# A fourth key block of the last batch moved from the projections into attention unit 3

## What is computed

```python
q = _heads(hidden_states @ to_q_w)
h_txt = _sdpa(q, _heads(ehs_txt @ to_k_w), _heads(ehs_txt @ to_v_w))
h_obj = _sdpa(q, _heads(ehs_obj @ to_k_object_w), _heads(ehs_obj @ to_v_object_w))
h_oth = _sdpa(q, _heads(ehs_oth @ to_k_others_w), _heads(ehs_oth @ to_v_others_w))
h_ip = _sdpa(q, _heads(ehs_ip @ to_k_ip_w), _heads(ehs_ip @ to_v_ip_w))
out = _merge(h_txt) + _merge(h_obj) + _merge(h_oth) + _merge(h_ip)
out = out @ to_out_w + to_out_b
out = (out + residual) / RESCALE
```

## Time and profile before

| what | us |
|---|---|
| median of 3 runs | 2387.88 (2387.11 to 2392.84) |
| the profiled execution | 2389.89 |
| its span | 2387.9 |
| PE busy | 2370.0 |
| ACT busy | 1777.2 |
| DVE busy | 1833.7 |
| POOL busy | 412.3 |

### The profile page before, as it was taken

The page is one execution under the profiler, slowest core; times in us unless marked ns, Lnnn a source line. Parts: engine busy times, 40 slices in busy tenths (PEclk is TensorE's granted clock), DMA queues, the critical chain, the costliest instruction groups (busy, mean ns, idle before and its releaser), DMA issues.

```text
span 2387.9 us, 37663 instructions
## 1 busy us (share of the span) xinstructions
PE 2370.0 (99%) x12801; PEld 1804.1 (76%) x12801; DVE 1833.7 (77%) x3291; ACT 1777.2 (74%) x3906; POOL 412.3 (17%) x564
## 2 busy tenths in 40 slices
PE   9999999999999999999999999999999999999999
PEld 8999999998999986566666666666666666666665
DVE  4457777632333479999999999999999999999994
ACT  4333433332222369999999999999999999999995
POOL 0000000000000023313223133133132232231310
PEclk9999999999999999999999999999999999999999
DMA  9545444385654577757777677676676776675762
GB/s 339 164 129 153 150 144 133 108 268 160 222 177 162 185 166 149 150 129 150 150 142 151 130 150 159 131 150 150 130 160 143 138 150 144 147 156 124 146 132 77
DMA packets 371750, 370.12 MB, mean 155 GB/s; under 512 B 110047, under 2 KB 298591, under 8 KB 371559
## 3 DMA queue, kind: packets, MB, share of 16 engines
q1 hardware_dynamic: 334384, 306.14, 56.2%
q10 hardware_dynamic: 37174, 61.59, 7.1%
HBM read 215.57 MB, written 83.89 MB: 125 GB/s over the span
## 4 chain that ended last, share of the span: by engine, by line
PE 96%; ACT 1%; DMA 1%; SPq 1%; issue 0%; DVE 0%; POOL 0%; ACTq 0%; POOLq 0%
PE st_ps L1660 17%; PE s_ps L489 13%; PE st_ps L509 12%; PE om_ps L523 12%; PE om_ps L544 11%; PE om_ps L567 10%; PE s_ps L1712 7%; PE om_ps L1712 4%; PE s_ps L1680 3%; PE st_ps L1712 3%; DMA qpack<-q_out 1%; PE om_ps L1729 1%; ACT s_ps L689 1%; PE om_ps L602 1%; ACT probs L681 1%; DMA xs_raw<-in_xT 0%
## 5 line engine op out<-in xcount | busy, mean ns | idle before, releaser
L689 ACT ACTIVATE s_ps<-s_ps,negmax 128x427 f32<-128x427 f32 x1280 | 768.1, 608 | 21.0 <-DVE small L758 20.9
L749 DVE TENSOR_REDUCE negmax<-s_ps 128x2 f32<-128x854 f32 x640 | 665.3, 1040 | 83.5 <-PE s_ps L489 77.1
L681 ACT ACTIVATE probs<-st_ps 128x1024 f32<-128x1024 f32 x632 | 656.3, 1038 | 21.9 <-PE st_ps L509 9.4
L489 PE MATMUL s_ps<-kpack,qpack 96*128 96x512 f32 x1280 | 422.2, 411 | 5.0 <-DMA qpack<-q_out 3.3
L509 PE MATMUL st_ps<-qpack,kpack 104*128 104x512 f32 x1264 | 404.9, 401 | 3.4 <-ACT probs L681 3.3
L447 POOL TENSOR_TENSOR small<-small,negmax 128x616 f32<-128x616 f32 x160 | 196.4, 1227 | 990.1 <-DVE negmax L766 990.0
L1660 PE MATMUL st_ps<-ctx_split,w_split_ip 128*128 128x428 f32 x1848 | 364.2, 357 | 0.0
L489 PEld LDWEIGHTS s_ps<-kpack,qpack 96*128 96x128 f32 x1280 | 223.6, 189 | 182.1 <-ACT s_ps L689 80.3
L1660 PEld LDWEIGHTS st_ps<-ctx_split,w_split_ip 128*128 128x128 f32 x1848 | 347.0, 188 | 15.6 <-issue 1.0
L544 PE MATMUL om_ps<-xs,wq 128*128 128x512 f32 x1200 | 342.6, 395 | 0.4 <-POOL xs L438 0.3
L567 PE MATMUL om_ps<-heads,wo 128*128 128x512 f32 x1125 | 320.7, 393 | 0.0
(11 more groups left out here) (116 smaller groups left out, 2436.8 us busy)
## 6 DMA issues: line engine op xcount, KB each, us to landing
qpack<-q_out SPq DMA_DIRECT2D x240, 256.0 KB, 6.8
kpack<-kT SPq DMA_DIRECT2D x240, 217.5 KB, 3.4
kT<-k_out ACTq DMA_DIRECT2D x154, 217.5 KB, 3.5
ctx_split_raw<-in_ctxT SPq DMA_DIRECT2D x128, 214.0 KB, 4.6
tok_pair<-in_ctxT SPq DMA_DIRECT2D x48, 512.0 KB, 4.7
xs_raw<-in_xT SPq DMA_DIRECT2D x85, 256.0 KB, 4.2
out<-in_xT SPq DMA_DIRECT2D x75, 256.0 KB, 4.8
out_yT<-out SPq DMA_DIRECT2D x75, 256.0 KB, 2.1
```

The source lines that it names most:

```text
L489: last = nc.tensor.matmul(s_ps[:, n % 2, z, :], qpack[r][0:ROWS_S, j, t * P:(t + 1) * P], kpack[r][0:ROWS_S, j, :], start=True, stop=True)
L681: nc.scalar.activation(probs[:, at:at + 2, :], transposed(u, duo), ACT.Exp).then_inc(p_done, 1)
L689: last = nc.scalar.activation(s_ps[:, n % 2, z, SMALL:TOK], s_ps[:, n % 2, z, SMALL:TOK], ACT.Exp, bias=negmax[:, r, IP, j, t:t + 1], accu ...
L749: nc.vector.tensor_reduce(negmax[:, r, IP, j, t0:t0 + 2], s_ps[:, n % 2, :, SMALL:TOK], AX_X, ALU.max, negate=True).then_inc(s_max, 1)
```

## The change

`DEFER` goes from 3 to 4: block m = 1 of the last batch joins m = 2, 3 and 4 as a late block, and slot 3 makes the last of them, in the same places as slots 1 and 2. `ORDER` is one step shorter and all first scores, queries and maxima stand one block earlier against the runs. Slot 3's queries use the common tables, and only slot 4 the `alone` ones. The loads and splits of Wo move one slot on. Of the splits, two stand ahead of the first subtraction of maxima in slot 4 and three ahead of the second. On ACT the first probability of unit 0 stands ahead of the second half of unit 1's small exponentials.

```diff
-DEFER = 3
+DEFER = 4
@@ LATE_KEYS
-             2: {0: (0, 6), 1: (6, 12), 2: (12, 18), 3: (18, 24)}}
+             2: {0: (0, 6), 1: (6, 12), 2: (12, 18), 3: (18, 24)}, 3: {0: (0, 6), 1: (6, 12), 2: (12, 18), 3: (18, 24)}}
@@ attention
-    from_late_weights = low + size([P, FIRST - 1, 2, TOK])
+    from_late_weights = low + size([P, 1, 2, TOK])
@@ sync_ops, slot
             if w > 0 and unit(w + 3):
                 pack_queries(w + 3)
+            if w == DEFER:
+                load_wo(range(3, QC))
             if w % QC == 1 and unit(w + 4):
                 load_x(w + 4, range(X_EARLY, QC))
...
             if w == DEFER - 1:
                 load_wo(range(0, 3))
             if w == DEFER:
-                load_wo(range(3, QC))
                 load_bias()
@@ pool_ops, slot
+            if w == DEFER:
+                split_wo(0)
+                split_wo(1)
             if unit(w + 2):
                 less_max(w + 2, 0)
...
-            for c in {3: (0, 1), 4: (3, 4)}.get(w, ()):
-                split_wo(c)
+            if w == DEFER:
+                for c in range(2, QC):
+                    split_wo(c)
             if unit(w + 2):
                 less_max(w + 2, 1)
-            if w == 3:
-                split_wo(2)
@@ act_ops, slot and rest
             for k in range(STEPS):
                 prob(w, k)
+                if (w, k) == (0, 0):
+                    small_exp(1, 1)
...
         def rest():
-            small_exp(1, 1)
             for w in range(UNITS):
                 slot(w)
```

## The result

The changed kernel takes 2393.7 us, the median of 21 runs (2388.8 to 2400.5), against 2387.6 for the kernel before on the same chip, also 21 runs (2382.4 to 2393.4). The ratio is 1.0027, 95% interval 1.0020 to 1.0035: about 6 us slower, within 0.3%. The forecast was 2392.3, range 2386.5 to 2398. The profiled execution took 2390.9 (span 2388.9), so it is one of the quicker ones of its kernel.

The account below looks back on a forecast made before the run. TensorE, busy in 99% of the span, was taken to bound the kernel. Terms of 0.9 + 1.2 + 0.8 + 0 - 1.4 + 2.6 + 0.3 = +4.4 us gave 2392.3, range 2386.5 to 2398.

Parts of the forecast that it names:

- Part 1: End of projections to unit 2's first scores: removing a block gains nothing; later release +0.9, store collision +1.2 us.
- Part 1, the release: End of run 18, which releases unit 2's kpack and qpack: later by two score pairs, +0.9 us.
- Part 1, chain and cover: From release to unit 2's first scores: chain 12.4 us, cover 6.5, so TensorE stands still for 5.9.
- Part 1, the store collision: Same chain: stores of one or two more finished key blocks compete, +1.2 us, between 0 and 3.0.
- Part 2: TensorE's restart after the head wait: low clock, +0.8 us, between a gain of 1.35 and a loss of 2.7.
- Part 3: Start of unit 0: first probability 0.66 us sooner, given back by a later maximum; 0, between -0.7 and +0.6.
- Part 4: Unit 3: unit 2's work and no Wo ahead of its qpack, 19.8 us instead of 21.23, -1.4.
- Part 5: Unit 4: inherits unit 3's stall from Wo loads ahead of qpack, +2.6 us, between 0 and +4.3.
- Rival C: Unit 4: late Wo pieces make GpSimd's splits the wait, 2395.9 or 2397.7 us instead of +0.3; chance 0.18.
- Rival B: Head: the cover is not needed, scores come 5.2 us sooner, 2384 or 2381 us in all; chance 0.06.
- Rival A: Head and unit 4: quicker queue, no store collision or clock cost, little or no stall, 2387 to 2389 us; chance 0.22.

Follow-up runs that it names:

- run 18: Not a follow-up: a run of projection matmuls inside the kernel, whose end releases unit 2's kpack and qpack transfers; complete at 865.92 us before, 868.9 in the changed kernel.
- Splits_early: Changed kernel with the context splits of the last two runs in three steps (2, 3, 3) instead of four: 2394.3 us, ratio to before 1.0024.
- Max_ahead: Changed kernel with GpSimd's second subtraction of unit 6 ahead of the last two Wo splits: 2394.4 us, ratio to before 1.0029.
- exp_first: Changed kernel with unit 1's small exponentials back ahead of the first probability: 2397.0 us, ratio to before 1.0034.
- prob_alone: Kernel before with only the first probability moved ahead of unit 1's small exponentials: 2386.0 us, ratio to before 0.9996.
- before_wo_behind: Kernel before with all five Wo loads directly behind slot 3's qpack and all splits in slot 4: 2388.5 us, ratio to before 1.0005.
- queries_ahead: Changed kernel with all fifteen query products ahead of unit 2's first scores: 2394.2 us, ratio to before 1.0030.

## Why the prediction was right, and where it was not

The time is right, 2392.3 against 2393.7. The sum is right partly by luck, because errors of opposite sign met. The profiles first: from the mark to the start of unit 7 the two executions of before take 793.9 and 789.9 (mean 791.9), the three of after 797.1, 796.8 and 797.1 (mean 797.0). That is +5.1, against +6.1 of the medians and +4.4 of the sum; the two of before lie 4 us apart, so it is good to about 2. The first profiles of each kernel alone give +3.2 there and +1.0 at the end, since the first of before also lost 1.5 us to two stray waits near 2230 (1.2 on qpack, 0.3 on GpSimd). The means by stretch:

| stretch | predicted | measured |
|---|---|---|
| mark to the first scores of unit 2 (part 1) | +2.1 | +3.2 |
| from there to the end of unit 0 (parts 2, 3) | +0.8 | +0.2 |
| unit 3 (part 4) | -1.4 | -0.3 |
| unit 4 (part 5) | +2.6 | +1.3 |
| GpSimd's splits, seen in unit 5 | +0.3 | +0.7 |

**Part 1, the release: the step that failed.** "The release itself comes later by the two score pairs that now lie ahead of it, +0.9" missed a wait. From the mark, run 18 completes 3.2 us later in the first execution, 0.9 from the two pairs and 2.0 from the 1.82 and what hangs on it (TensorE's first to eighth score pair takes 17.66 instead of 15.62); 0.3 stays open. In the second execution it is 4.7, with a low clock behind the wait. The order of the instructions showed the splits directly behind the small maxima; I looked there for a late block at the head and found it harmless, and did not ask what GpSimd does in that moment 36 us earlier. Splits_early shows that the place of the splits is the cause, though it brings back 1.0 only, with new waits of 0.36 and 0.32.

**Part 1, chain and cover.** Right to a microsecond. Predicted were a chain of 12.4 us, a cover of 6.5 and a wait of 5.9. Measured: 12.35, 11.5 and 11.5 us from release to first scores, and 5.5, 4.6 and 4.6 us of waits in it (4.61, 3.75 and 3.72, plus 0.85 on late splits each time), so the wait on qpack alone is below the 5 to 8 us that were to show it. The estimate of 5.6 us by the fit of the Trainium skill ("DMA: Bandwidth & Descriptors") was far off. Its section gives the fit per transfer and for transfers that GpSimd issues ("Anatomy of one DMA — SWDGE (gpsimd) path"); here SyncE issues nine (six kpack, not three, and three qpack), the last of them 4 us after the release, and qpack landed 5.8 to 8.1 us after its issue. The DMA engines were busy all the while, yet moved 139 GB/s while the qpack copies ran. Why these copies are slow was not tested.

**Part 1, the store collision, +1.2.** Not there. The stores went out inside the chain, one block's at 869.69 and two at 875.53, as expected, but the chain was no longer for it. That made up for part of the missed 2.0 us. First scores of unit 2 from the mark: 651.7 and 651.5 before, 654.9, 655.5 and 653.9 after, so +3.2 where 0.9 + 1.2 = 2.1 was predicted.

**Part 2, the clock, +0.8.** Right in kind, smaller on average. Behind the head wait the clock was low in all three executions (882 to 884 in the first). Max_ahead, which is the same kernel up to there, had none, and took 23.28 us from first scores to the end of unit 0, against 24.50 to 24.81: one stretch costs 1.2 to 1.5. The kernel before has such a stretch in its first execution (cost 1.5) and not in the second. So the term is between -0.3 and +1.5 by execution, and +0.6 in the mean of the three against the two.

**Part 3, first probability, 0.** Right for the changed kernel beside exp_first, where the second step takes back what the first gains. In the kernel before it is -0.4, within the bounds, with the maximum moved as predicted. Max_ahead, without a low clock, took 0.35 less from the first scores to the end of unit 0 than the second execution of before (23.28 against 23.63), so the gain may be there in the changed kernel too when the clock is high; no run separates it.

**Part 4, unit 3, -1.4.** Unit 3 takes 19.90 to 19.92 in every execution, 19.8 was predicted. What was wrong is the base. The 21.23 of the earlier trace rows was a wait of 1.82 with a low clock behind it, and the second execution has 19.13, and four other kernels without the late block have 18.6, one of them (prob_alone) with the queue of the kernel before. A late block costs a unit 1.3 us, which the stall of one execution had hidden. The term lies between -1.3 and +1.3. The size came from one execution, and I took it for a property of the kernel.

**Part 5, unit 4, +2.6, between 0 and 4.3.** Right in mechanism: the stall moves on, with the wait and the late landings, and before_wo_behind shows that Wo ahead of qpack makes them late. Its size came from the same single execution. Over the eight executions unit 4 takes 18.61 to 23.88, on average 20.5 against 18.6, +1.9 (the three of the changed kernel itself: +1.3). The highest is 1.0 beyond the bound, because a wait of 3.94 has the low clock behind it. What was to make the upper end, Wo loads directly behind qpack slowing it, is not seen where it stands alone (before_wo_behind). The ring order of the Trainium skill did not rule that end out either: the same section ("Queues, rings and completion order") adds that a later descriptor may finish its write before an earlier one.

**Rival C, GpSimd as the bound of unit 4, +0.3.** Present in small. ScalarE waited 1.05 us for the subtraction, and unit 5 takes 19.2 to 19.8 instead of 18.65 where unit 4's qpack wait is short, and 18.6 to 18.7 where it is 2 us or more, since the two delays overlap. That is +0.65 in the mean of three. Rival B is out: the head wait is there in every execution of the changed kernel. Rival A is out by its time, 2387 to 2389, though its conditions came true in part: the stores did not lengthen the chain, and unit 4's transfer was once in time but for 0.17.

## What to carry to other kernels

A stretch of independent work ahead of a transfer's first use is cover; take it away and all of it is lost, however little the wait behind it shows, so measure the chain from its release to its use before moving anything out of it. Before a row becomes a term, look at a second execution: the wait and the low clock of unit 3 were 2.6 us of one execution and 0.5 of the next. And put GpSimd's operations on SBUF where VectorE has no operation with two SBUF inputs or a cast: moving five splits gave back 3.2 us of two units in the profile.

## What was not expected of the hardware

- VectorE and GpSimd, when they meet on SBUF, cost each other more than their own length suggests: small VectorE operations of 0.22 to 0.28 us took 0.63 to 1.67 beside GpSimd instructions of 0.7 and 1.56 us, and GpSimd's 0.32 took 0.68. That fits waiting for the other's whole instruction, as the Trainium skill has it ("SBUF — State Buffer", section "SBUF: two separate sides").
- A TensorE wait of 1 to 4 us was often followed by some 3 us (10 in queries_ahead) at the 1.2 GHz level, costing another 1.2 to 1.6: after the 1.82 in the projections in one execution of three, after the head wait in all executions of the changed kernel but not in max_ahead, after 1.07 in before_wo_behind. So a wait of TensorE has two prices, and which one is paid differs by execution. Whether this makes the 10 us by which a kernel's times scatter was not tested.
- Left open: the three qpack copies might be issued sooner if unit 2's pack lay clear of the context splits in memory. That needs the memory laid out anew and was not tried.
